# Layer 0's later attention scores from three bfloat16 parts with a constant bias

## What is computed

```python
# layer 0: differential attention; 16 heads, two maps of 4 dims each
q, k = (t.reshape(Bm, Nm, 2 * H, hd).transpose(0, 2, 1, 3) for t in (q, k))   # hd = 4
def sdpa(qh, kh):
    scores = jnp.einsum('bhqd,bhkd->bhqk', qh, kh) * scale                     # 4 ** -0.5
    a = jax.nn.softmax(scores, axis=-1)
    return jnp.einsum('bhqk,bhkd->bhqd', a, v)
o = sdpa(q1, k1) - lam * sdpa(q2, k2)
...
x = x + attention0(xn) + ffn0(xn)      # ffn0: block-quantised matmul
x = x + attention1(xn) + ffn1(xn)      # layer 1: rope, 16 heads of 8 dims; three +-1 matmuls
```

## Time and profile before

| | |
|---|---|
| median of 3 runs | 862.29 us (862.2 to 862.35) |
| the profiled execution | 863.47 us, its span 861.7 us |
| mean granted TensorE clock | 0.991 |
| PE, ACT, DVE, POOL busy | 823.4, 761.9, 543.8, 35.9 us |
| DMA moved | 74.85 MB, mean 87 GB/s |

### The profile page before, as it was taken

The page is one execution under the profiler, slowest core; times in us unless marked ns, Lnnn a source line. Parts: engine busy times, 40 slices in busy tenths (PEclk is TensorE's granted clock), DMA queues, the critical chain, the costliest instruction groups (busy, mean ns, idle before and its releaser), DMA issues.

```text
span 861.7 us, 17309 instructions
## 1 busy us (share of the span) xinstructions
PE 823.4 (96%) x6751; PEld 286.6 (33%) x6751; DVE 543.8 (63%) x1200; ACT 761.9 (88%) x610; POOL 35.9 (4%) x56
## 2 busy tenths in 40 slices
PE   8899899999999999999999999999998999999997
PEld 6223223342333233332333323333232333333332
DVE  6877874857574686656674765747768276277322
ACT  3989889989889998899889998899988899899986
POOL 4100000000000100001000010000100000000000
PEclk9989999999999999999999999999999999999999
DMA  3817447602538025560357314481153702401500
GB/s 104 175 41 143 103 85 175 90 1 75 135 82 122 14 75 136 126 78 13 114 116 136 47 51 127 95 136 19 62 154 81 124 6 100 97 2 74 135 13 14
DMA packets 42448, 74.85 MB, mean 87 GB/s; under 512 B 6552, under 2 KB 8216, under 8 KB 42360
## 3 DMA queue, kind: packets, MB, share of 16 engines
q1 hardware_dynamic: 40560, 68.12, 36.7%
q0 software_dynamic: 1744, 5.44, 2.1%
q10 hardware_dynamic: 56, 0.10, 0.0%
HBM read 36.84 MB, written 35.65 MB: 84 GB/s over the span
## 4 chain that ended last, share of the span: by engine, by line
PE 65%; ACT 23%; DVE 6%; issue 5%; DMA 0%; DVEq 0%; ACTq 0%; SPq 0%
PE ps_pv L972 28%; ACT probs L721 22%; PE ps_s L954 17%; PE ps_misc L804 7%; PE ps_misc L800 7%; PE ps_misc L805 5%; PE ps_misc L793 1%; DVE pv_sb L1449 1%; ACT ff_out L734 0%; ACT ff_out L736 0%; DMA q_ab<-shifts 0%; DVE xn L1076 0%; DVE q_ab L1301 0%; DVE tmp L1067 0%; DVE stat L1069 0%
## 5 line engine op out<-in xcount | busy, mean ns | idle before, releaser
L721 ACT ACTIVATE probs<-ps_s 128x1536 f32<-128x1536 f32 (+1 forms) x522 | 722.8, 1431 | 59.2 <-PE ps_s L954 57.9
L972 PE MATMUL ps_pv<-probs,v_aug 128*32 128x512 f32 x3072 | 413.6, 611 | 13.6 <-ACT probs L721 6.9
L954 PE MATMUL ps_s<-q_ab,k_ab 18*128 18x512 f32 x1024 | 175.4, 499 | 8.5 <-ACT probs L721 7.6
L954 PEld LDWEIGHTS ps_s<-q_ab,k_ab 18*128 18x128 f32 x1024 | 65.4, 182 | 216.1 <-issue 113.5
L1201 DVE CAST h_hi<-ff_out 128x512 fp32r<-128x512 f32 x64 | 27.4, 427 | 112.7 <-ACT ff_out L734 110.0
L972 PEld LDWEIGHTS ps_pv<-probs,v_aug 128*32 128x32 f32 x3072 | 61.5, 108 | 110.5 <-issue 90.7
L954 PE MATMUL ps_s<-q_c,k_c 32*128 32x512 f32 x512 | 87.2, 495 | 4.4 <-ACT probs L721 4.1
L804 PE MATMUL ps_misc<-h_hi,k_w 128*128 128x512 f32 x192 | 85.9, 448 | 0.3
L1449 DVE STREAM_TRANSPOSE pv_sb<-ps_pv 128x512 f32<-128x512 f32 x48 | 34.4, 717 | 73.4 <-PE ps_pv L972 70.5
L805 PE MATMUL ps_misc<-h_lo,k_w 128*128 128x512 f32 x192 | 75.8, 395 | 0.0
L954 PEld LDWEIGHTS ps_s<-q_c,k_c 32*128 32x128 f32 x512 | 32.6, 181 | 106.9 <-ACT probs L721 67.6
(11 more groups left out here) (167 smaller groups left out, 552.0 us busy)
## 6 DMA issues: line engine op xcount, KB each, us to landing
parts_dram<-qk_parts SPq DMA_DIRECT2D x94, 256.0 KB, 3.7
parts_dram<-qk_parts SPq DMA_DIRECT2D x16, 512.0 KB, 2.8
q_c<-parts_dram SPq DMA_DIRECT2D x32, 256.0 KB, 5.0
...
```

Source lines behind the costliest of these rows:

```text
L721: ins = nc.scalar.activation(probs[:, tr.probs + a:tr.probs + b], ps_s[:, tr.banks + a:tr.banks + b], ACT.Exp, bias=-SCALE[1] * BOUND[1] i ...
L954: ins = nc.tensor.matmul(ps_s[:, tr.banks + i, :], k[row:row + n, slot, c * P:(c + 1) * P], q[row:row + n, slot, :], start=True, stop=True)
L972: ins = nc.tensor.matmul(ps_pv[32 * j:32 * j + 32, :], v_aug[:, U.v, c, a:a + 32], probs[:, (4 * S + j) % PROBS, :], start=c == 0 and not ...
```

## The change

- In layer 0 with b from 1, q and k are split into three bfloat16 parts (`qk_thirds`). DVE makes the first from PSUM and the remainder `qk_rest` in float32; GpSimd makes the second part and the third (`split_rest`), as its items at `q0` and `k0`.
- Eight rows for each of the 4 dims, so 32 rows in a row group, in `q_ab` and `k_ab`, now bfloat16: products 1x1, 1x2, 2x1, 1x3, 3x1, 2x2, 2x3 and, in the last place, 3x2. `write_thirds` writes seven of the places, `write_last_third` the last one after `exact0`, since the exact bias, where it is needed, takes that place.
- No bias rows for b from 1: `load_shift`, the two memsets of `exact0` and `shift_loaded` go for these units; the exp gets the constant bias -30, as layer 1's has one.
- Sequence 0 (A0, B0) keeps float32r parts and shifts, now in `q_c` and `k_c`. The four constant DMAs of ones on ACT's queue become eight.
- `Triple.runs` splits an exp also where the bias changes (between B0 and A1).
- SP's order: A1 and B1 are loaded one behind the other without waiting for scores of A1; C0 waits for B0's scores. `exact_max` has a third way for the three parts (taken only if the bound does not hold).
- The order of dims and heads in the projection's weights changes with it (`g l` for `l g`).

Cut to its core:

```diff
+THIRDS = 3
+THIRD_ROWS = 8 * DQK[0]
+Q_PLACES = ((0, slice(0, 3)), (1, slice(3, 6)), (2, slice(6, 7)))
+K_PLACES = ((0, slice(0, 7, 3)), (1, slice(1, 5, 3)), (2, slice(2, 6, 3)))
+LAST_PLACE, LAST_PART = 7, (2, 1)
...
+        self.first = self.layer == 0 and self.b == 0
+        self.bias = 0.0 if self.first else -SCALE[self.layer] * BOUND[self.layer]
...
-        q_ab = sb("q_ab", [P, 8, N], F32R)
-        k_ab = sb("k_ab", [P, 8, N], F32R)
+        q_ab = sb("q_ab", [P, 8, N], BF16)
+        k_ab = sb("k_ab", [P, 8, N], BF16)
...
+        def write_thirds(eng, b, i):
+            times = 2 * (b - 1) + i + 1
+            eng.wait_ge(thirds_made, THIRD_OPS * times)
+            eng.wait_ge(rest_split, THIRD_OPS * times)
+            n = P // MAPS[0]
+            for m in range(MAPS[0]):
+                r = slice(n * m, n * (m + 1))
+                for a, at in (Q_PLACES, K_PLACES)[i]:
+                    dst = thirds_of(b, i)[m, at].rearrange("a p n -> p a n")
+                    eng.dma_start(dst, qk_thirds[r, i, a].unsqueeze(1).broadcast_to([n, dst.shape[1], N])).then_inc(thirds_written[i], 16)
+
+        def write_last_third(eng, b):
+            eng.wait_ge(shift_ops[2], SHIFT_OPS[2] * b)
+            for i in range(2):
+                for m in range(MAPS[0]):
+                    eng.dma_start(thirds_of(b, i)[m, LAST_PLACE], qk_thirds[r, i, LAST_PART[i]]).then_inc(thirds_written[i], 16)
...
             writes(0, 1)
-            scores_done(unit("B", 0))
+            write_last_third(sp, 1)
             load_qk(unit("A", 1))
-            load_shift(sp, unit("A", 1))
-            scores_done(unit("A", 1))
-            load_shift(sp, unit("B", 1))
+            load_qk(unit("B", 1))
             writes(0, 2)
-            load_qk(unit("B", 1))
+            write_last_third(sp, 2)
             writes(1, 0)
             write_last(sp, 0)
+            scores_done(unit("A", 1))
             load_qk(unit("C", 0))
...
             writes(0, 7)
+            write_last_third(sp, 7)
             scores_done(unit("B", 6))
             load_qk(unit("A", 7))
-            load_shift(sp, unit("A", 7))
...
+            def split_rest(b, i):
+                times = 2 * (b - 1) + i
+                pool.wait_ge(thirds_made, THIRD_OPS * (times + 1))
+                nc.gpsimd.tensor_copy(qk_thirds[:, i, 1], qk_rest[:]).then_inc(rest_split, 1)
+                pool.wait_ge(rest_split, THIRD_OPS * times + 1)
+                nc.gpsimd.tensor_tensor(qk_thirds[:, i, 2], qk_rest[:], qk_thirds[:, i, 1], ALU.subtract).then_inc(rest_split, 1)
...
-                                               bias=-SCALE[1] * BOUND[1] if layer == 1 else 0.0, scale=SCALE[layer])
+                                               bias=tr.tiles[a].U.bias, scale=SCALE[layer])
...
-                act.dma_start(k_ab[r:r + PARTS, 2:8].bitcast(F32), ff_out[0:PARTS * 6]).then_inc(k_ones_loaded, 16)
+                act.dma_start(k_c[r:r + PARTS, 0:4].bitcast(F32), ff_out[0:PARTS * 4]).then_inc(k_ones_loaded, 16)
+                act.dma_start(k_c[r:r + PARTS, 6:8].bitcast(F32), ff_out[0:PARTS * 2]).then_inc(k_ones_loaded, 16)
...
-                        parts_free(0, i)
-                        nc.vector.tensor_copy(hi, ps).then_inc(split_ops[0], 1)
-                        dve.wait_ge(split_ops[0], base + 1)
-                        ins = nc.vector.tensor_tensor(lo, ps, hi.bitcast(F32), ALU.subtract)
+                        if b > 1:
+                            dve.wait_ge(thirds_written[i], THIRDS_WRITTEN * (b - 1))
+                        nc.vector.tensor_copy(qk_thirds[:, i, 0], ps).then_inc(thirds_made, 1)
+                        wait(dve, rest_split, THIRD_OPS * times)
+                        dve.wait_ge(thirds_made, THIRD_OPS * times + 1)
+                        nc.vector.tensor_tensor(qk_rest[:], ps, qk_thirds[:, i, 0], ALU.subtract).then_inc(thirds_made, 1)
...
-                    else:
-                        nc.vector.memset(sh[0].bitcast(F32), -BOUND[0]).then_inc(shift_ops[0], 1)
-                        nc.vector.memset(sh[1].bitcast(F32), 0.0).then_inc(shift_ops[0], 1)
```

More of the change, by code:

```diff
@@ L206, in __init__ @@
         self.v = (0 if self.b in (0, 7) else 1) if self.layer == 0 else 1 if self.b in (5, 7) else 0
-        self.stack = "CD"[self.b % 2] if self.layer == 1 else self.kind
-        self.times = self.b // 2 if self.layer == 1 else self.b
+        self.first = self.layer == 0 and self.b == 0
+        self.bias = 0.0 if self.first else -SCALE[self.layer] * BOUND[self.layer]
+        if self.layer == 1:
+            self.stack, self.times, self.rows = "CD"[self.b % 2], self.b // 2, ROWS[1]
+        elif self.first:
+            self.stack, self.times, self.rows = self.kind + "0", 0, ROWS[0] + PARTS
+        else:
+            self.stack, self.times, self.rows = self.kind, self.b - 1, THIRD_ROWS
 class Triple:
@@ L220, in runs @@
     def runs(self):
-        layers = [tile.U.layer for tile in self.tiles]
-        cut = next((i for i in range(1, 3) if layers[i] != layers[0]), 3)
-        return [(a, b, layers[a]) for a, b in ((0, cut), (cut, 3)) if a < b]
+        kinds = [(tile.U.layer, tile.U.bias) for tile in self.tiles]
+        cut = next((i for i in range(1, 3) if kinds[i] != kinds[0]), 3)
+        return [(a, b, kinds[a][0]) for a, b in ((0, cut), (cut, 3)) if a < b]
 class Tile:
@@ L448, in operands @@
         def operands(U):
-            q, k = (q_c, k_c) if U.layer == 1 else (q_ab, k_ab)
-            return q, k, (4 if U.stack in "BD" else 0), 4
+            q, k = (q_c, k_c) if U.layer == 1 or U.first else (q_ab, k_ab)
+            return q, k, (4 if U.stack in ("A0", "B", "D") else 0), 4
         def flag_of(layer, b):
@@ L550, in writes @@
                 for i in range(2):
-                    write(sp, layer, b, i, range(MAPS[layer]), parts_written[layer][i])
+                    if layer == 0:
+                        write_thirds(sp, b, i)
+                    else:
+                        write(sp, 1, b, i, [0], parts_written[i])
             def load_weights():
@@ L939, in operands_there @@
                     pe.wait_ge(qk_loaded[U.stack], loaded(U))
-                    if U.layer == 0:
-                        pe.wait_ge(shift_loaded[U.stack], SHIFTED * (U.times + 1))
+                    if U.first:
+                        pe.wait_ge(shift_loaded[U.stack], SHIFTED)
             def scores(tr):
@@ L951, in scores @@
                     q, k, slot0, _ = operands(U)
-                    n = ROWS[U.layer] + (PARTS if U.layer == 0 else 0)
+                    n = U.rows
                     row, slot = TILE_ROWS * j, slot0 + g
@@ L1386, in exact_max1 @@
                     base, made = GEN_USES[1] * b, GEN_MADE[1] * b
-                    row_maxima(1, b, base, made)
+                    row_maxima(1, b)
                     done = base + T * n + 1
@@ L1569, in _ @@
             nc.vector.memset(shifts[:, 1, :].bitcast(F32), 0.0).then_inc(ones_made, 1)
-            for layer in range(2):
-                dve.sem_inc(gen_taken[layer], 1)
+            for way in range(3):
+                dve.sem_inc(gen_taken[way], 1)
             setup_first()
```

254 lines of the change are left out of this document (163 added, 91 removed).

## The result

The changed kernel takes 849.66 us (median of four runs, 849.02 to 853.43), the kernel before, run beside it, 862.25. The ratio is 0.987, 95% interval 0.984 to 0.990: 12.6 us faster. The forecast was 857.2, its range 849 to 867. The profiled execution took 849.02 us, its span 847.2.

A forecast was written before the change was run, and what follows sets the result against it. PE was taken as the bound, 65% of the chain, layer 0's scores 17%. -14.0 (score groups) + 0.2 (split exp) + 7.3 (late operands) + 1.4 (clock) = -5.1 us, giving 857.2 us, range 849 to 867.

The forecast's parts named there:

- second rival: First groups of A1 and A7: operands come in time, 0.8 us late at A7 only; 849.3 us, chance 0.11.
- The saving of a score group: Layer 0's score groups: weight load 67 ns shorter with bfloat16, 14.0 us saved in all (0 to 21).
- good end: Weight load of the score groups: shrinks to the 95 ns of the 32-column bfloat16 record, 87 less than 182.
- first rival: Score groups' weight load shrinks to the 95 ns row, 18.1 us saved; 853.1 us, chance 0.26.
- the 245 groups: Layer 0's score groups with b from 1: 245 of the 299 that the change touches lie on the path.
- the 85%: Share of the score groups' saving taken to arrive, since ACT ends the wait each time PE catches up.
- The matmul record unchanged: Score groups: the matmul record stays as it is, float32r already taking one pass; only the weight load shortens.
- GpSimd's operations "at nothing": GpSimd's copy (0.61 us) and subtraction (1.27) after q0 and k0: no part in the chain, no cost.
- The late operands: First groups of A1 and A7: PE stands still 3.2 and 4.1 us for loads, 7.3 together (0 to 17).
- the four steps: From k0's second pass to A1's and A7's rows: GpSimd 2.0, k writes 4.9, last third 3.6, loads 9.5; 20.0 us.
- the prediction's own last sentence: Wrong if spacing falls below 0.3, no DMA ends a wait at A1 and A7, or a GpSimd wait is in the chain.
- The clock after a wait: Behind the waits at A1 and A7 the clock is lower for a while: 1.4 us lost (0 to 4).

The follow-up runs named there:

- type alone: Kernel before with only layer 0's score operands in bfloat16, two parts, third left out, no work on GpSimd: 840.18 us against 863.33, ratio 0.974.
- GpSimd beside: Kernel before with bfloat16 score operands in two parts, plus a copy and a subtraction on GpSimd that nothing waits for: 849.27 us, ratio 0.981.
- run with late loads: Changed kernel with six small transfers on SP's queue between the loads of q and k for A1 and A7: 863.55 us in one run.
- without GpSimd: Changed kernel without GpSimd's two operations, second and third parts being zeros set once at the start: 844.13 us, ratio 0.978.
- B6's standstill was shortened: Changed kernel with `quant_mm` at step 13 in the loop and B6's quantisation steps 5 and 6 behind `exact0`: 843.85 us, ratio 0.977.
- the bias put off: Changed kernel with the take and regrouping of A6's sums in B6 ahead of sequence 7's bias and quantisation: 855.33 us, ratio 0.990.
- the later order: Kernel before with only `quant_mm` at step 13 in the loop and B6's quantisation steps 5 and 6 behind `exact0`: 865.67 us, ratio 1.003.

## Why the prediction came out as it did

The time fell at the low edge of the range, near the second rival's 849.3, but not by the forecast's terms. Two terms were too small, in opposite directions, and one was not there. The saving was 9.1 us short (14.0 for 23.1) and GpSimd's price 9.1 short (nothing for 9.1); that the two cancel, and the time still lies in the range, is luck. From the runs: -23.1 (type alone) + 9.1 (GpSimd beside) + 0.4 (all the rest: third part, loads, order, eight constant DMAs) = -13.6 us, against -12.6 measured; the kernel before had medians of 862.25 to 863.33 beside these runs, which is the size of the difference. B0's 1.3 us in the first term and 1.2 in the second, which the change has neither of, cancel in it.

**The saving of a score group: mechanism right, size too small.** It took the middle between the line by bytes (132 ns) and the short bfloat16 load (95 ns), which is 68.5 ns less, not 67, or 0.3 us in the sum; the load is 91 ns with all 128 columns, under the good end. The spacing shrank by 0.11 us, not 0.067: more than the record, and the first rival had the better row. 245 x 0.11 x 0.85 = 22.9. The type alone gave 23.1, of which B0 has 1.3 outside the 245 groups, so the product of the count and the 85% is near; neither is shown by itself. Behind that stands the Trainium skill's rule that the prediction weighed (TensorE: Matmul & The Clock Gate, section Weight-path perf modes); on the load the trace agrees with it, 91 against 181 ns.

"The matmul record unchanged" was wrong, 385 ns against 499, and why the record shrank no run shows. But no pass was saved. In the run with late loads, at the lower clock, a bfloat16 group holds PE for 0.54 us:

```profile
91.20 0.61 PE L1043 MATMUL ps_s<-q_ab,k_ab 32*128 32x512 bf16 x3
91.74 1.94 PE L1061 MATMUL ps_pv<-probs,v_aug 128*32 128x512 f32 x8
```

That is 0.22 more than 0.32, and by the prediction's own working one pass of 512 columns is 0.21 more.

**GpSimd's operations "at nothing": the step that failed.** Its durations were near (607 and 1418 ns, for 0.61 and 1.27), and it is in no chain, as forecast. By that place in the chain the prediction priced it, and gave it no effect on DVE's operations; the price was there. DVE's own 6% of the chain, which looked like room, was of a PE with 0.43 us groups, and it was a mean over units: in B6 PE already waited for the take. The runs put it at 9.1 us; it is shown by addition (beside) and by removal (5.5 us, without GpSimd). Two things between these numbers the traces show: the 1.6 us that the zeros cost at the start, and the 1.2 us in B0, which the changed kernel doesn't have. The rest I leave open; single executions of one kernel lie between 0.4 and 8.9 us apart.

**The late operands: a sound chain, with sizes too large, and its effect hidden.** From the end of k0's second pass at 66.68 to the last landing at 82.8 there were 16.1 us at A1, not 20.0. Three of the four steps came in their ranges: GpSimd 2.3 us (2.0 forecast), the writes of k 4.4 (4.9), the last third up to the first load 2.9 (3.6). The mis-sized term is the loads, 6.6 us for 9.5 (8.4 to 11.5). The loads of A1 (issue in ns, then landing in us):

```profile
L575 SPq DMA_DIRECT2D q_ab<-thirds_dram x4: 339/423/430, 76.2 to 77.5; - x4
L575 SPq DMA_DIRECT2D k_ab<-thirds_dram x4: 307/416/632, 78.4 to 79.9; - x4
...
DMA to landing us min/median/max: 2.6/2.9/3.1
```

An issue is 0.42 us, not 0.6, and a landing 2.9, not 5.0. And the prediction had their packets wrong: it took them as 1 KB, where they are 4 KB. The order `g l` puts the four heads of a row side by side in DRAM. Between 81 and 86 us, when only these loads run, no packet lies between 512 B and 2 KB:

```profile
DMA packets 446, 1.23 MB, mean 247 GB/s; under 512 B 148, under 2 KB 148, under 8 KB 445
```

The 297 packets over 2 KB carry 1.22 MB, 4.1 KB each: 32 a load, where the kernel before has 64 of 2 KB. The Trainium skill's rule (DMA: Bandwidth & Descriptors, section Why small descriptors are slow), a fixed cost for each packet, thus favours the change, and the prediction had it on the wrong side; the trace doesn't speak against it. How much of the earlier landing the packets explain stays open: in the type alone 64 packets of 1 KB to 16 partitions, half the bytes, land after 2.7 us at the same place.

PE went on at A1 without a gap: a product of 0.61 us from 82.87, the first group at 83.42. By the prediction's own last sentence it is wrong there. Yet at A7 the wait existed, 2.8 us once B6's standstill was shortened, and 4.1 with the bias put off. It isn't the change's alone: in the kernel before it is 1.9 us with the later order. The second rival came true at both places in the changed kernel, at one of them only because another wait came first.

**The clock after a wait: too small.** 1.4 us for 7.3 of waiting; the run with late loads lost 6.2 for 7.0, beyond the upper end of 4.

**The rest.** C units unchanged at 30.0 us, ACT's part of the chain up, the split exp and the memsets free: as forecast. A0's 1.3 us of gain are not the change's: the clock fell after the same wait in the profile of before, and not in that of after, and the kernel before takes 34.7 us there too in the profile of the later order.
